# Node pass: the last multiply of each tile on GpSimd between its gathers, instead of on VectorE

## The reference

```
x = layernorm(x + L0(x, edge_attr, src, dst, eps))            # (1 + eps) x + sum over edges of relu(x[src] + edge)
x = layernorm(x + L1(x, edge_weight, src, dst))               # ten steps of weighted propagation
x = layernorm(x + L2(x, norm, weight1, weight2, bias1, bias2, src, dst, edge_type))
x = layernorm(x + L3(x, theta, phi, src, dst))                # segment_max over incoming edges, 0 where there are none
```

## Time and profile before

| | |
|---|---|
| median of 3 runs | 4459.67 us (4459.03 to 4461.9) |
| the profiled execution | 4465.7 us, span 4463.9 us |
| node pass, first load to last multiply | 266.9 to 758.3 us of the span |
| first gather of the following stage | 769.55 us |
| busy in the whole span | VectorE 67%, GpSimd 58%, TensorE 56%, ScalarE 28% |

### The profile page before, as it was taken

The page is one execution under the profiler, slowest core; times in us unless marked ns, Lnnn a source line. Parts: engine busy times, 40 slices in busy tenths (PEclk is TensorE's granted clock), DMA queues, the critical chain, the costliest instruction groups (busy, mean ns, idle before and its releaser), DMA issues. The chain is left out here.

```text
span 4463.9 us, 60648 instructions
## 1 busy us (share of the span) xinstructions
PE 2502.3 (56%) x9482; PEld 1176.3 (26%) x9482; DVE 2971.8 (67%) x7710; ACT 1232.9 (28%) x3893; POOL 2610.8 (58%) x2544
## 2 busy tenths in 40 slices
PE   4720000677777588888888487561222104995654
PEld 2510000333333244344444222111111101333332
DVE  7989997988888488788888586332332234663333
ACT  0023332332232255445554222111000012441111
POOL 4747772655554477764444564774565613656776
PEclk9965555887777799899999799785555557995555
DMA  6647776888887866675555476333434243332111
GB/s 223 229 119 211 219 217 182 154 152 147 149 149 133 153 173 162 164 164 145 142 142 133 120 208 171 71 57 59 49 49 45 34 99 84 73 68 40 36 37 27
DMA packets 628412, 557.12 MB, mean 125 GB/s; under 512 B 379089, under 2 KB 548122, under 8 KB 623330
## 3 DMA queue, kind: packets, MB, share of 16 engines
q1 hardware_dynamic: 477606, 418.72, 34.7%
q0 software_dynamic: 90112, 95.44, 16.7%
q10 hardware_dynamic: 60612, 42.15, 3.5%
HBM read 291.63 MB, written 290.82 MB: 130 GB/s over the span
## 5 line engine op out<-in xcount | busy, mean ns | idle before, releaser
L1302 POOL DMA_INDIRECT out<-xob,ob x400 | 412.0, 1030 | 358.7 <-DVE xob L1414 251.8
L278 POOL DMA_INDIRECT gb<-nodes,ib x400 | 396.5, 991 | 348.9 <-ACT ib L855 249.6
L491 POOL DMA_INDIRECT xdst<-in_x,dstc x400 | 457.0, 1142 | 226.4 <-issue 135.1
L262 PE MATMUL bank<-ident,act 128*99 128x128 f32 x400 | 84.6, 348 | 666.2 <-DVE act L999 649.4
L298 PE MATMUL bank<-chosen,rec 128*6 128x512 bf16 x1200 | 370.0, 473 | 0.9 <-DVE chosen L285 0.9
L278 POOL DMA_INDIRECT cgb<-layer,ib x160 | 175.6, 1098 | 232.3 <-ACT ib L2193 185.9
L1341 PE MATMUL bank<-hm,w 128*48 128x512 f32 x600 | 296.0, 632 | 0.0
L1358 PE MATMUL bank<-bxT,w 105*128 105x512 f32 x600 | 283.2, 608 | 8.7 <-ACT bxT L1245 8.6
L272 PE MATMUL bank<-ident,scan 99*128 99x99 f32 (+2 forms) x1120 | 199.5, 308 | 152.1 <-DVE scan L2012 101.5
L291 PE MATMUL bank<-l_chosen,l_rec 128*3 128x512 f32 x480 | 250.6, 672 | 0.3 <-DVE l_chosen L285 0.3
L278 POOL DMA_INDIRECT parent<-upper_rows,ib x176 | 176.1, 1000 | 119.1 <-ACT ib L1270 54.6
(11 more groups left out here) (292 smaller groups left out, 6764.8 us busy)
## 6 DMA issues: line engine op xcount, KB each, us to landing
nodes<-wt SPq DMA_DIRECT2D x40, 1286.2 KB
edges<-gb ACTq DMA_DIRECT2D x100, 194.0 KB, 5.9
upper_rows<-tb SPq DMA_DIRECT2D x100, 194.0 KB, 4.9
xa<-upper_rows SPq DMA_DIRECT2D x100, 194.0 KB, 3.0
lsb<-edges SPq DMA_DIRECT2D x100, 194.0 KB
run_rows<-upper_rows SPq DMA_DIRECT2D x100, 194.0 KB, 4.3
deep_sum<-zeros SPq DMA_DIRECT2D x20, 960.0 KB, 21.6
layer<-zeros SPq DMA_DIRECT2D x20, 960.0 KB, 25.1
```

The costliest lines, as they stand in the source:

```text
L262: last = nc.tensor.transpose(slot(dst_ps[0:w, :], t), rows_sb[:, t, c0:c0 + w], ident[:, :])
L278: yield nc.gpsimd.indirect_dma_start(out=dst[s][:, t, 0:width], out_offset=None, in_=table, in_offset=bass.IndirectOffsetOnAxis(ap=ib[s][: ...
L491: nc.gpsimd.indirect_dma_start(out=xdst[:, k * F:(k + 1) * F], out_offset=None, in_=a["x"], in_offset=bass.IndirectOffsetOnAxis(ap=dstc[:, ...
L1302: nc.gpsimd.indirect_dma_start(out=out, out_offset=bass.IndirectOffsetOnAxis(ap=ob[s][:, t:t + 1], axis=0), in_=xo[s][:, t, :], in_offset= ...
```

## The change

The multiply that writes `no` moves from VectorE to GpSimd. The [125, 20] factor, so far in `nr4`, gets two buffers of its own (`nro`), and a semaphore `s_ro` tells GpSimd that it is written. GpSimd's 68 groups are dealt out over the 40 tiles in whole groups: one group (4 gathers) or two groups (8 gathers) stand ahead of each multiply, 12 times one and 28 times two. `s_o`, which says that `no` is written and which SyncE's store waits for, is now counted up by GpSimd. It also protects `nd` and `nro`: VectorE waits for it in `center`, between the sum and the instruction that overwrites `nd`, and in `fourth_of` ahead of writing `nro`. The wait for the store of the tile two back (`s_ow`) moves to GpSimd with the multiply.

```diff
+            nro, s_ro = [sc(f"nro{b}", [HP, ROWS]) for b in range(2)], scope.sem("n_ro")
...
                 def _(pool):
-                    for g in range(EARLY, NG):
-                        fetch_dst(g, s_late)
+                    for n in range(CHUNKS):
+                        b, late = n % 2, NG - EARLY
+                        for g in range(EARLY + n * late // CHUNKS, EARLY + (n + 1) * late // CHUNKS):
+                            fetch_dst(g, s_late)
+                        pool.wait_ge(s_ro, n + 1)
+                        wait(pool, s_ow[b], 32 * (n // 2))
+                        nc.gpsimd.tensor_tensor(no[b][:, :, :], nd[b][:, :, :], mid(nro[b][:, :], ROWS), ALU.mult).then_inc(s_o, 1)
                     pool.wait_ge(s_late, NG * 16 * T)
...
-                    ch = {k: Chain(dve, z, n) for k, z, n in ((1, s_a1, 1), (3, s_a3, 3), (4, s_a4, 3), (6, s_a6, 2), (7, s_a7, 2))}
+                    ch = {k: Chain(dve, z, n) for k, z, n in ((1, s_a1, 1), (3, s_a3, 3), (4, s_a4, 3), (6, s_a6, 2), (7, s_a7, 1))}
...
                         ch[1].then(nc.vector.tensor_reduce(nm[:, :], nx[s][:, :, :], AX.X, ALU.add))
+                        wait(dve, s_o, n - 1)
                         nc.vector.scalar_tensor_tensor(out=nd[b][:, :, :], in0=mid(nm[:, :], ROWS), scalar=-1.0 / F, in1=nx[s][:, :, :], op0=ALU.mult, op1=ALU.add).then_inc(s_c1, 1)
...
                         ch[7].then(nc.vector.reciprocal(nr4[:, :], ns4[:, :]))
-                        ch[7].then(nc.vector.tensor_tensor(nr4[:, :], nr4[:, :], nr3[:, :], ALU.mult))
-                        wait(dve, s_ow[b], 32 * (i * 2 + s // 2))
-                        nc.vector.tensor_tensor(no[b][:, :, :], nd[b][:, :, :], mid(nr4[:, :], ROWS), ALU.mult).then_inc(s_o, 1)
+                        wait(dve, s_o, n - 1)
+                        nc.vector.tensor_tensor(nro[b][:, :], nr4[:, :], nr3[:, :], ALU.mult).then_inc(s_ro, 1)
```

## The result

The changed kernel takes 4489.44 us (median of 3 runs, 4484.67 to 4491.42) where the kernel before takes 4459.67: the ratio is 1.0063, with a 95% interval of 1.0041 to 1.0086. It is 28 us slower by the ratio (the medians lie 29.8 us apart). The direction and the range of the forecast held; its size, +42 us, was half as much again too large.

A forecast was written before the change was run, and what follows sets the result against it. VectorE was taken to pace the node pass. 39 turns longer by 0.98 us gave 38 us, plus 1 for the last multiply and 3 for queue gaps: +42, from 4459.7 to 4502 us, range 4452 to 4542.

The forecast's parts named there:

- Part 1: VectorE's node pass: removing L763 saves 1.08 us a turn, 43 us over 40, with nothing else late at that point.
- Part 2: Length of the multiply on GpSimd: 2.1 us, between bounds of 0.92 and 3.05 us.
- Part 3: VectorE after the factor: GpSimd's multiply and two-input instructions exclude each other, so the 1.08 us are given back every turn.
- Part 4: GpSimd's own turn: 14.15 us with 8 gathers and the multiply, 8.25 with 4; 13.0 us a turn on average.
- (b): Turn with GpSimd 1.25 us late: the multiply falls between L773 and L774 or behind L774; turn 12.8 us.
- (c): Turn with GpSimd 3.75 us late: multiply ends at 5.85 us after the factor; turn 12.9, early again after 4 gathers.
- step (d): Once in ten turns, a third piece of 8 gathers: GpSimd 4.85 us late, turn 14.0 us.
- The last multiply: End of the node pass: 1 us added because the final multiply takes 2.1 us for 1.16.
- The long gaps: Gaps of 8.0 and 3.5 us in GpSimd's queue, no longer covered by its lead: 3 us added, bounds 0 and 11.5.
- VectorE isn't held: Rival: only GpSimd waits, so its own pace gives 12.6 us a turn, +24 us, 4484; chance 0.12.
- A short multiply: Rival: multiply at the lower bound of 0.92 us, 11.3 us a turn, -28 us, 4432; chance of faster 0.15.
- no change: Rival: effects cancel with GpSimd's multiply near 1.4 to 1.6 us; chance 0.08.

The follow-up runs named there:

- e5: Changed kernel with four nd buffers, GpSimd's multiply placed beside the sums, six gathers ahead of each multiply and EARLY = 42: 4449.32 us, ratio 0.9974.
- e9: Changed kernel with all gathers in the counting stage and GpSimd copying nd into no instead of multiplying: one execution, turn 11.90 us.
- e1: Kernel before and changed kernel, each with all gathers in the counting stage: ratios to the kernel before 1.0678 and 1.0677.
- e7: Changed kernel with EARLY = 42 and six gathers ahead of each multiply, buffers and waits as changed: 4480.73 us, ratio 1.0046.
- e3: Changed kernel with the large multiply back on VectorE, its gather dealing and waits kept: 5117.61 us on another chip, ratio 1.0032.
- e6: Kernel before with EARLY = 42 in place of 32, moving 40 gathers into the counting stage: 4475.9 us, ratio 1.0036.
- e11: Against the changed kernel: GpSimd multiplies only even tiles, beside the sums, four nd buffers, EARLY = 36, up to 13 gathers per multiply: 4446.9 us, ratio 0.9970.

## Why the prediction was right, and where it was off

- **What bounds** (VectorE paces, a change of the pass moves the end one to one): right. All of the loss stands in the pass, +30 us.
- **Part 1** (43 us taken from VectorE): right, and e5 shows that most of them can be had, 33 us over its turns. "Nothing else comes late" held at that point of the turn only: with L763 gone VectorE waits longer for ScalarE's square ahead of the second sum (25.6 us in e5, 35.9 in e9, 19.2 before). In the changed kernel the hold covered that wait instead (19.2 us to 3.4), which the sum had left out: a term of -16 us that I missed.
- **Part 2** (2.1 us): mis-sized. The multiply takes 1.80 us, near the 1.7 us that the sum by IOTA rows gives if the write hides behind the reads. The estimate by the Trainium skill, GPSIMD Engine Reference, section 3.1, 2.1 us by scaling, is too high for this shape, in which one input repeats each value 48 times; the measurement decides, and no run shows whether the repeated input is the reason. So 0.3 us too much stands in the hold and in GpSimd's turn alike.
- **Part 3** (mutual exclusion gives the 1.08 us back at every turn): right in kind, shown by e1 and e7. I named L772 as the first held instruction, because I had only seen two-input instructions hold gathers. It was the `tensor_scalar` ahead of it, which reads one tensor. For the length of the hold this made little: 1.5 us against the 1.83 that the sum had in it. The step's own result, a turn of 12.9 us when GpSimd is on time, measured 12.0 (e1) to 12.15 (e7), and 12.03 in the changed kernel (factor at 324.81, the next at 336.84). This is the term that was mis-sized most: the hold is 0.3 us shorter, since the multiply is, and ScalarE's wait of 0.5 us is gone. Another 0.1 us a turn, some 4 us in all, is a slip of the sum: its steps start from the one turn shown, 12.11 us, and are compared with the mean, 12.02.
- **Part 4** (GpSimd's pace decides in turns of 8): right for the changed kernel. The rows give 12.67 us for such a turn (300.41 to 313.08 in the changed kernel), for 12.8 to 12.9 in steps (b) and (c). That it would bind without the hold is not shown. The 1.9 us of waits for a piece of 8 measured 1.0 here, because the gathers fall into step with the multiply. Lateness didn't add up as in step (d): the turn behind a third eight in a row takes 12.66 and 12.65 us (399.90 to 412.56 and 656.12 to 668.77), for 14.0, and 13.5 only behind the long gap. Step (b)'s choice between two places for a late multiply didn't arise: VectorE was held ahead of the multiply's shown start, so that VectorE stayed in step with GpSimd.
- **The sum**: 39 x 0.98 = 38 us measured 22.8. The last multiply, +1, measured +4.8, since I had put GpSimd on time there. The long gaps, +3, are inside these 22.8: behind a gap of 7.28 us in GpSimd's queue stand the three waits of L732 (5.5, 2.9 and 3.0 us), and those three turns take 42.7 us where three pieces of eight in a row took 38.0 before (374.5 to 412.6), +4.7. So the steps alone, 38 us, measured some 18. The total came nearer than its parts: the gap, the last multiply and the tail, 12 us together for the 4 foreseen, made up for part of it. The tail of 2.5 us for late gathers (9.6 us in e3) was missing.
- **The rivals**: *VectorE isn't held* is excluded by e1. *A short multiply*: at 1.80 us it wasn't short. The point that I gave for no change, 1.4 us, was too high: in e9, with 0.99 us in that place and no gathers beside it, the turn only reaches that of the kernel before, through the hold and ScalarE's square together.

The rule behind part 3 was that whichever starts first holds the other for its whole instruction. In both directions one engine waits for the other: gathers for VectorE, VectorE for the multiply (1.69 us for 0.19) until 0.04 to 0.06 us after its end. The order of the starts fits where GpSimd is on time. Behind a gather it doesn't: L777 starts 0.5 us ahead of the multiply's shown start and is held all the same. The Trainium skill, SBUF — State Buffer, "Who interferes with whom", also says that `tensor_scalar` can enter a mode that uses both ports while sums (`tensor_reduce`) never contend; here the `tensor_scalar` was held (2272 ns for 186) and the sums weren't (1.15 us in e5). By that page L777 was a candidate ahead of L772.

## What to carry to other kernels

An elementwise operation on GpSimd is not free for VectorE: count its whole length as a hold on VectorE's next instruction that reads two tensors or is a `tensor_scalar`, unless it runs beside sums. To gain by it, place it there (more buffers, and a wait for the right instruction), and count GpSimd's own turn with all its gathers, since a multiply that comes late leaves the free place and holds again: the pass only became shorter when both were done. Then look for the next wait, here ScalarE's square. And a row of a small instruction whose duration has grown tenfold is a wait that the profile counts as busy time.

## What the runs showed of the hardware that was not expected

- A multiply of GpSimd that stands behind a gather holds VectorE before its own shown start: L777 starts at 312.56 and is held until the end of a multiply that is shown from 313.08 on (2.38 us), while it is held for 1.69 us where GpSimd had been waiting. Whether the multiply takes what they share when it is issued, or its shown start is late, can't be told from these rows.
- A copy of 960 elements takes GpSimd 987 ns and a multiply with a repeated second input 1.80 us; VectorE's multiply takes 1.158 us.
- Gathers late in a block cost at its end: 20.9 us from the last multiply to the next stage in e3, against 11.3 us when they are long done (the kernel before, and e1 on the chip of e3).
- Forty more gathers in the counting stage cost it 16.7 us (e6), sixteen more nothing (e11). GpSimd's idle time at the stage's end is 45.3 us in the kernel before, 24.5 with sixteen more and 6.5 with forty more: a gather there costs it 1.3 to 1.4 us, and forty no longer fit.
